# Two layer transformer on one core: the experts' first tiles among self attention's last pieces, and GpSimd's subtractions in parts

## The chip, the cores and the metric

One core of a Trainium2 chip runs the program. The time is the device time of the execution in microseconds; the median of three runs of the kernel before is 2374.72 us (2372.3 to 2374.88).

## What is computed

Two decoder layers over 8 x 256 = 2048 tokens of width 512 in float32, each sublayer followed by a residual addition and a layer norm. The change lies in the first layer, whose sublayers are:

```python
x = _layernorm(x + _L0_attn_ref(x, ...))            # power attention, 16 query heads of 128, 8 key heads
x = _layernorm(x + _L0_xattn_ref(x, ctx, ctx))      # causal cross attention, 16 heads of 32
x = _layernorm(x + _L0_ffn_ref(x, ...))             # router, 8 basis experts, shared expert

# power attention: a = (q k / sqrt(128)) ** 2, masked and gated; y = a v / sum(a); y @ Wc + bc
# _L0_ffn_ref:
gate, up = (xt @ w_gate).reshape(T, K, I), (xt @ w_up).reshape(T, K, I)      # K = 8, I = 256
basis = jax.nn.silu(gate) * up
mixed = jnp.einsum('tek,tki->tei', mix_sel, basis)                           # top 4 of 128 routes
out = ... (mixed @ w_down weighted by coeff) + silu(xt @ sgate) * (xt @ sup) @ sdown
```

The second layer is another attention, a quantised cross attention and small experts. The change doesn't touch it.

## The kernel before, in words

Every float32 product is made of three float32r products: an operand is split into a high part (a copy to float32r, mostly on ScalarE) and a low part (the operand minus its high part, on VectorE or GpSimd), and high x high, high x low and low x high are summed in PSUM (`pair3`). Names end in H and L for these parts.

Three stages of the first layer share the engines: `attention0` (A), `cross0` (C) and `experts0` (X). Each stage is a set of five generators, one for each engine, that yield after every tick. `decoder` writes an order of ticks by hand, the same for all five engines, as pairs (stage, number of ticks); `beside` mixes ticks of a second stage into those of a first. So every engine executes its instructions in that order, and semaphores tie the engines together. PSUM's eight banks are handed out in the same order, to the piece whose bank has been free longest (`Rooms`); self attention's second half and the experts' ticks before 76 use banks 0 to 3, cross attention 4 to 7. A piece waits until the last reader of its bank is done.

Self attention (A) runs 32 steps n, one per key head and quarter of 512 tokens, eight ticks each: three projections (`project`, L384), the output pieces of step n-2 in two ticks (`out`, L417, added by VectorE at L653), the attended product of step n-1 (`attend`, L434 to L439, divided at L664) with value projections now and then, the scores (L471, L473; squared at L597, multiplied with the gates at L710) and the transposition of step n-1's result (`turn`, L486; split at L605 and L722). Norms of 4 x 128 tokens are taken where their additions end: statistics (L191 to L199), Newton steps of 128x4 numbers (L203 to L213), and the apply on ScalarE (L240) or, in cross attention, on VectorE (L219). Steps 32 and 33 only finish steps 30 and 31. GpSimd makes the low parts of the weights (QKL L771, VL L791, CL L784), gates (E, L757 to L767), and residual additions (L779).

Cross attention (C) runs eight batches of 20 ticks (12 idle ticks between batch 3 and 4): scores (L953), maxima (L1069), exponentials (L1037, L1039), their transposition (`flip`, L965; copied at L1048), the product with values (L936), a last transposition (`finish`, 23 ticks behind), the product with the denominators (L1095), GpSimd's addition (L1137), and the norm.

The experts (X) run 160 tiles u of 128 tokens x (256 gate + 256 up) columns: two halves of 8 token tiles, each over ten weights (two shared, eight basis). Tile: 12 matmuls (L1289), tanh or Silu on ScalarE (L1421, L1423), two products on VectorE (L1470, L1484 or L1487); for basis weights GpSimd adds into `mixed` (L1586). Weight w is copied by ScalarE (WH, L1405) and subtracted by GpSimd (WL, L1590) at tick 8(w-1)+1; the first one at tick -5. `turn` (L1328) transposes four token tiles, split at L1436 and L1539, at ticks -2, -1, 76 and 80. Results of the shared weights and of `mixed` are transposed (`flip`, L1316, split at L1428 and L1533) and multiplied with `w_down` (`out`, L1305, added at L1528), one tick apart: the output piece is two ticks behind its tile, three for `mixed`.

The experts' buffers lie over self attention's in SBUF. Before tick -2 they use the first 32 KB, free when the last projection is done (`second_half`); at tick -2 every engine waits for all that self attention still does (`self_ends`):

```python
K.second_half = qk_mm.upto(3 * N), v_mm.upto(4 * NT)
K.self_ends = (o_mm.upto(4 * N), t_hi.upto(2 * N), o_add.upto(4 * N), e_in.upto(2 * N), ...)
```

The order around the seam is: step 31 mixed with batch 3's last ticks, step 32, X -6, step 33 up to its output pieces, X -5 to -3, the rest of step 33, X -2 to 0, then 76 experts' ticks with batches 4 to 7 beside them.

## Time and profile before

| | us |
|---|---|
| profiled execution | 2378.91 |
| its span, first to last instruction | 2377.1 |
| TensorE matmuls busy | 2108.7 (89%) |
| VectorE busy | 1305.2 (55%) |
| ScalarE busy | 1060.7 (45%) |
| GpSimd busy | 796.7 (34%) |
| mean granted TensorE clock | 0.950 of full |

The profile is one execution. A row names line, engine and operation, out<-in by the program's names, shapes and durations; behind it stands how long the engine was idle before and what ended that. PE is TensorE, DVE VectorE, ACT ScalarE, POOL GpSimd, SP SyncE. Self attention alone runs to about 450 us, with cross attention to about 850, the last steps to 900, the experts with cross attention to 1245 and alone to 1555; the second layer follows.

### The profile page before, as it was taken

The page shows a single profiled execution, that of the slowest core. Times are in us where ns is not written, and L with a number is a line of the kernel's source. Part 1 is how long each engine was busy: PE and PEld are TensorE (multiplying, and loading weights), DVE is VectorE, ACT ScalarE, POOL GpSimd, SP SyncE. Part 2 cuts the span into 40 slices and gives each one's busy share as a digit, 9 for nine tenths or more (in the row PEclk, how much of TensorE's full clock was granted, in tenths as well). Part 3 has the DMA queues.
Part 4 walks back from the last instruction along what each step waited for, and adds up shares of the span by engine and source line. Part 5 has one row for each costly group of instructions (what it writes and reads, how often), then busy time and mean ns, then how long its engine had stood idle before and what let it go on. Part 6 is the DMA issues. An engine that isn't in the chain of part 4 may idle for free.

```text
span 2377.1 us, 37602 instructions
## 1 busy us (share of the span) xinstructions
PE 2108.7 (89%) x13655; PEld 1672.7 (70%) x13669; DVE 1305.2 (55%) x3333; ACT 1060.7 (45%) x2367; POOL 796.7 (34%) x679
## 2 busy tenths in 40 slices
PE   7899999898999978999999999968999778888764
PEld 6788888687878856877777888755555367666442
DVE  2554545544465456545456411356777676777555
ACT  3332332444444424445533312145666557777632
POOL 1743533333343222134431134254445231322100
PEclk9899999899999988999999999979999889999886
DMA  3311112011012012011110011033324210000001
GB/s 132 126 36 63 45 35 73 18 58 47 27 49 62 19 36 71 25 52 48 33 50 18 18 54 74 7 52 54 61 49 62 87 41 28 15 19 6 1 10 71
DMA packets 57878, 109.03 MB, mean 46 GB/s; under 512 B 7136, under 2 KB 35040, under 8 KB 54112
## 3 DMA queue, kind: packets, MB, share of 16 engines
q1 hardware_dynamic: 57696, 106.63, 15.4%
q8 instruction: 111, 1.82, 0.3%
q14 instruction: 71, 0.58, 0.1%
HBM read 86.10 MB, written 4.26 MB: 38 GB/s over the span
## 4 chain that ended last, share of the span: by engine, by line
PE 39%; DVE 10%; issue 7%; ACT 4%; POOL 2%; SPq 1%; DMA 1%; ACTq 0%; DVEq 0%; POOLq 0%
PE PS L1289 17%; PE PS L1880 3%; PE PS L1784 3%; PE PS L1305 2%; DVE st L191 2%; ACT xP L2545 2%; DVE aM L2020 1%; PE PS L1848 1%; PE PS L953 1%; PE PS L1868 1%; PE PS L965 1%; DVE PS L2667 1%; PE PS L1835 1%; ACT xN L240 1%; PE PS L1891 1%
## 5 line engine op out<-in xcount | busy, mean ns | idle before, releaser
L1289 PE MATMUL PS<-WH,bXH 128*128 128x512 f32 x640 | 258.7, 404 | 0.0
L1289 PE MATMUL PS<-WH,bXL 128*128 128x512 f32 x640 | 250.3, 391 | 0.0
L1289 PE MATMUL PS<-WL,bXH 128*128 128x512 f32 x640 | 250.2, 391 | 0.0
L2020 DVE TENSOR_REDUCE aM<-PS 128x4 f32<-128x1024 f32 x128 | 153.8, 1221 | 55.2 <-PE PS L1848 54.0
L384 PE MATMUL PS<-aXH,QKH 128*128 128x512 f32 x384 | 158.9, 414 | 14.6 <-ACT sq L597 8.4
L1586 POOL TENSOR_TENSOR mixed<-mixed,s 128x256 f32<-128x256 f32 x112 | 82.4, 739 | 245.5 <-DVE s L1487 245.3
L1590 POOL TENSOR_TENSOR WL<-sg,WH 128x2048 fp32r<-128x2048 f32 x20 | 92.1, 4604 | 186.5 <-ACT WH L1405 186.5
L384 PE MATMUL PS<-aXH,QKL 128*128 128x512 f32 x384 | 154.3, 402 | 0.0
L384 PE MATMUL PS<-aXL,QKH 128*128 128x512 f32 x384 | 154.0, 401 | 0.0
L1959 ACT ACTIVATE aPT<-PS 128x1024 f32<-128x1024 f32 x128 | 128.6, 1024 | 49.8 <-PE PS L1868 49.0
L684 DVE TENSOR_TENSOR qkL<-PS,qkH 128x512 fp32r<-128x512 f32 x96 | 65.9, 690 | 141.1 <-ACT qkH L561 141.0
L1289 PEld LDWEIGHTS PS<-WH,bXH 128*128 128x128 f32 x640 | 120.7, 189 | 28.5 <-issue 2.0
L1289 PEld LDWEIGHTS PS<-WH,bXL 128*128 128x128 f32 x640 | 120.4, 188 | 26.5
L1289 PEld LDWEIGHTS PS<-WL,bXH 128*128 128x128 f32 x640 | 120.8, 189 | 22.8
L653 DVE TENSOR_TENSOR xN<-PS,xN 128x512 f32<-128x512 f32 x128 | 88.2, 691 | 78.7 <-PE PS L417 76.3
L2545 ACT ACTIVATE xP<-PS,xM 128x256 f32<-128x256 f32 x256 | 118.0, 482 | 29.0 <-DVE xM L2667 29.0
L710 DVE TENSOR_TENSOR aT<-sq,E 128x512 f32<-128x512 f32 (+1 forms) x128 | 84.4, 701 | 82.3 <-ACT sq L597 44.0
L757 POOL TENSOR_SCALAR E<-lgB,lgS 128x256 f32<-128x256 f32 x64 | 74.2, 1160 | 157.0 <-DVE aT L710 147.5
L1487 DVE SCALAR_TENSOR_TENSOR s<-s,cf,PS 128x256 f32<-128x256 f32 x112 | 53.9, 481 | 127.4 <-ACT s L1423 125.4
L561 ACT ACTIVATE qkH<-PS 128x512 fp32r<-128x512 f32 x96 | 57.0, 599 | 137.3 <-PE PS L384 137.3
L1470 DVE SCALAR_TENSOR_TENSOR s<-s,PS 128x256 f32<-128x256 f32 x80 | 33.7, 421 | 148.7 <-ACT s L1421 148.6
L597 ACT ACTIVATE sq<-PS 128x768 f32<-128x768 f32 x64 | 52.0, 812 | 140.4 <-PE PS L473 87.4
(395 smaller groups left out, 6038.1 us busy)
## 6 DMA issues: line engine op xcount, KB each, us to landing
sg<-in_gu SPq DMA_DIRECT2D x16, 1024.0 KB, 4.8
gQK<-in_Wqk SPq DMA_DIRECT2D x16, 768.0 KB, 6.2
gC<-in_Wc SPq DMA_DIRECT2D x16, 512.0 KB, 7.0
lgB<-gate_sums SPq DMA_DIRECT2D x32, 256.0 KB, 4.6
aqs<-aQH SPq DMA_DIRECT2D x64, 128.0 KB, 4.1
xN<-in_xT SPq DMA_DIRECT2D x4, 1024.0 KB, 11.1
xN<-in_x SPq DMA_DIRECT2D x4, 1024.0 KB, 7.7
cst<-in_cT SPq DMA_DIRECT2D x8, 512.0 KB, 4.0
```

The lines of the kernel that those rows point to most:

```text
L384: mm = e.matmul(PS[:, b, :], w[:, kc, 128 * m:128 * m + 128], x[:, kc, c:c + 512], start=kc == 0 and i == 0, stop=kc == KC - 1 and i == 2)
L653: e.tensor_tensor(xN[:, t, :], PS[:, b, :], xN[:, t, :], ALU.add).then_inc(o_add.sem, 1)
L710: at = e.tensor_tensor(aT[:, j, c:c + w].rearrange("p (h q) -> p h q", h=2), sq[:, c:c + w].rearrange("p (h q) -> p h q", h=2), E[:, j:j + ...
L757: e.tensor_scalar(E[:, j, 0:256], lgB[:, n % 2, 256 * j:256 * j + 256], lgS[:, c0:c0 + 1], 0.0, ALU.subtract, ALU.min)
L1289: mm = e.matmul(PS[:, b, :], x[:, kc, c:c + 128], y[:, kc, :], start=kc == 0 and n == 0, stop=kc == KC - 1 and n == 2)
L1586: e.tensor_tensor(mixed[:, i, :], mixed[:, i, :], s2[tick % 2][:, :], ALU.add).then_inc(t_add.sem, 1)
L1590: e.tensor_tensor(WL[w % 2][:, :, :], sg[:, :, :], WH[w % 2][:, :, :].bitcast(F32), ALU.subtract).then_inc(w_lo.sem, 1)
L1784: mm = e.matmul(PS[:, b, 0:256], w[:, kc, 128 * m:128 * m + 128], x[:, kc, :], start=kc == 0 and k == 0, stop=kc == KC - 1 and k == 2)
L1880: mm = e.matmul(PS[32 * r:32 * r + 32, b, :], V[y][:, kt, 4 * i + r, :], PT[:, (n + 2 * (r // 2) + kt) % 8, r % 2, :], start=kt == 0, stop ...
L1959: e.activation(PT[:, n % 8, :, :], PS[:, b:b + 2, :], ACTF.Exp, scale=0.25).then_inc(t_exp.sem, 1)
L2020: e.tensor_reduce(M[j % 2][:, :, :].rearrange("x q (h c) -> x h q c", h=2)[:, :, :, i], PS[:, b:b + 2, :].rearrange("p h (q k) -> p h q k" ...
L2545: last = e.activation(P[:, i % 2, a, q, :], PS[:, r, 256 * q:256 * q + 256], ACTF.Exp, bias=M[y][:, q, h:h + 1], scale=-1.0, accum_out=den ...
```

## The change

1. Self attention's buffers are laid out by when they fall free: those free after the last projection first (112,128 bytes), then the split queries and keys, free after the last scores, then gates, squares, powers and values, free after the last attended product, then the turned output and its weights. The experts' buffers are laid over them in four groups, and the common wait at tick -2 is replaced by one for each group, where it is first used: `projected`, `scored`, `attended`, `self_out`. The down weights lie in two buffers, DH[0], DH[1].
2. The order of the seam: step 31's three projections, then all of batch 3's last ticks; then step 31's rest, 32 and 33 with X -4 to 4 among them. Tiles 0 to 4 so come before self attention's end, tile 0 ahead of step 30's output pieces, tile 1 among the last attended products. The experts' first transposition is at tick -3, ahead of the last scores, the second at tick 1.
3. The first weight's split is at tick -2, between the last scores and the transposition of step 30; the second weight's at tick 5 (was 1).
4. Output pieces of the experts come one tick later behind their tiles (three, four for `mixed`), norms of the experts' tokens too (80, 84, 160; were 79, 83, 159). The stage ends two ticks later.
5. Batches 4 to 7 start five experts' ticks later and end at tick 74 instead of 73; their last ticks go in pairs. Batch 7's `finish` and statistics are behind tile 72 (were behind 69 and 70), seed and Newton steps behind tile 73 (were behind 71 and 72), the apply behind tile 74 (was 73).
6. GpSimd's low parts are made in parts: QKL, VL and WL in four, CL, DL and each half of cKL in two instructions. VL is cut to 4 x 256 columns, QKL to 4 x 384, WL to 4 x 512.

```diff
@@ -280,21 +280,24 @@
     V[0] = W("V0", [128, 8, 2, 130])
     W = Places(K, 44160)
     XH[1], XL[1] = W("aXH1", [128, KC, 1024], F32R), W("aXL1", [128, KC, 1024], F32R)
-    V[1] = W("V1", [128, 8, 2, 130])
-    gQK, gV, gC = W("gQK", [128, KC, 384]), W("gV", [128, KC, 264]), W("gC", [128, 2, 512])
-    QKH, QKL = W("QKH", [128, KC, 384], F32R), W("QKL", [128, KC, 384], F32R)
-    VH, VL = W("VH", [128, KC, 264], F32R), W("VL", [128, KC, 264], F32R)
-    CH, CL = W("CH", [128, 2, 512], F32R), W("CL", [128, 2, 512], F32R)
+    gQK, QKH, QKL = W("gQK", [128, KC, 384]), W("QKH", [128, KC, 384], F32R), W("QKL", [128, KC, 384], F32R)
+    gV, VH, VL = W("gV", [128, KC, 264]), W("VH", [128, KC, 264], F32R), W("VL", [128, KC, 264], F32R)
+    bc = W("bc", [128, 512])
+    lg, lz, l1, UT = W("lg", [128, NT * 8]), W("lz", [128, NT * 8]), W("l1", [128, NT * 8]), W("UT", [128, 128])
+    assert W.at == K.floor + 112128
     qkH, qkL = W("qkH", [128, 3, 512], F32R), W("qkL", [128, 3, 512], F32R)
+    assert W.at == K.floor + 124416
     E = W("E", [128, 2, 384])
     sq = W("sq", [128, 768])
     aT = W("aT", [128, 2, 768])
+    V[1] = W("V1", [128, 8, 2, 130])
+    assert W.at == K.floor + 145024
     yN = W("yN", [128, 2, 2, 2, 128])
+    gC, CH, CL = W("gC", [128, 2, 512]), W("CH", [128, 2, 512], F32R), W("CL", [128, 2, 512], F32R)
     yH, yL = W("yH", [128, 2, 512], F32R), W("yL", [128, 2, 512], F32R)
-    lg, lz, l1 = W("lg", [128, NT * 8]), W("lz", [128, NT * 8]), W("l1", [128, NT * 8])
-    UT, DM = W("UT", [128, 128]), W("DM", [128, 2, 128])
+    assert W.at == K.floor + 169600
+    DM = W("DM", [128, 2, 128])
     lgS, lgR, lgB = W("lgS", [128, NT * 8]), W("lgR", [128, 128]), W("lgB", [128, 2, 512])
-    bc = W("bc", [128, 512])
     nr, nr2 = W("nr", [128, 2, 2, 1]), W("nr2", [128, 2, 2, 1])
     xst = [xN[:, 4 * p:4 * p + 4, :] for p in range(NP)]
@@ -768,8 +771,9 @@
                 if n % 2 and n // 2 + 1 < 16:
                     e.wait_ge(*in_qk.upto(n // 2 + 2))
                     e.wait_ge(*qk_hi.upto(n // 2 + 2))
-                    e.tensor_tensor(QKL[:, :, :], gQK[:, :, :], QKH[:, :, :].bitcast(F32),
-                                    ALU.subtract).then_inc(qk_lo.sem, 1)
+                    for kc in range(KC):
+                        last = e.tensor_tensor(QKL[:, kc, :], gQK[:, kc, :], QKH[:, kc, :].bitcast(F32), ALU.subtract)
+                    last.then_inc(qk_lo.sem, 1)
             yield
             if n < NP:
...
@@ -851,8 +857,8 @@
         yield
 
     K.first_half = qk_mm.upto(3 * 16), v_mm.upto(before[4]), y_mm.upto(2 * 16)
-    K.second_half = qk_mm.upto(3 * N), v_mm.upto(4 * NT)
-    K.self_ends = (o_mm.upto(4 * N), t_hi.upto(2 * N), o_add.upto(4 * N), e_in.upto(2 * N), c_lo.upto(16), y_mm.upto(2 * N), t_lo.upto(2 * N))
+    K.projected = qk_mm.upto(3 * N), v_mm.upto(4 * NT), residual.upto(NT)
+    K.scored, K.attended, K.self_out = s_mm.upto(2 * N), y_mm.upto(2 * N), o_mm.upto(4 * N)
     return Stage(8 * (N + 2) + 3, banks, tensor, scalar, vector, gpsimd, sync)
 
...
-    U, first, last = 160, -6, 163
-    outs = [(80 * h + 8 * k + i, 80 * h + 8 * k + i + (3 if k == 9 else 2), i, c, z)
-            for h in (0, 1) for z, (k, c) in enumerate(((0, 2), (1, 4), (9, 0))) for i in range(8)]
+    U, first, last = 160, -4, 165
+    outs = [(80 * h + 8 * k + i, 80 * h + 8 * k + i + (4 if k == 9 else 3), i, z)
+            for h in (0, 1) for z, k in enumerate((0, 1, 9)) for i in range(8)]
     out_at, flip_at = {}, {}
-    for v, (u, at, i, c, z) in enumerate(outs):
+    for v, (u, at, i, z) in enumerate(outs):
         out_at.setdefault(at, []).append(v)
     route_at, choose_at, gate_at, coef_at, mix_at = {}, {}, {}, {}, {}
     for p in range(NP):
         base, q = 80 * (p // 2), p % 2
@@ -1205,13 +1221,13 @@
             gate_at[base + 3 + 4 * q + k] = p, k
         choose_at[base + 2 + 4 * q] = p
         coef_at[base + 10 + 2 * q], mix_at[base + 11 + 2 * q] = p, p
-    split_at = {-5: 0}
-    for w in range(1, 20):
+    split_at = {-2: 0, 5: 1}
+    for w in range(2, 20):
         split_at[8 * (w - 1) + 1] = w
-    down_at = {0: 0, 4: 1, 12: 2}
+    down_at = {2: 0, 4: 1, 12: 2}
     norm_at = {}
     for p in range(NP - 1):
-        n = 79 + 80 * (p // 2) + 4 * (p % 2)
+        n = 80 + 80 * (p // 2) + 4 * (p % 2)
         norm_at.update({n: ("stats", p), n + 1: ("newton", p), n + 2: ("apply", p)})
     loads = [12 * (w // 10) + (2 * (w % 10) + 2 if w % 10 < 2 else w % 10 + 3) for w in range(20)]
 
...
@@ -1370,9 +1387,6 @@
             mm.then_inc(f_mm.sem, 1)
 
         for tick in range(first, last):
-            if tick == -2:
-                for x in old:
-                    e.wait_ge(*x)
             if 0 <= tick < U:
                 tile(tick)
@@ -1393,23 +1407,25 @@
 
     def scalar(e):
         for tick in range(first, last):
-            if tick == -5:
+            if tick == -2:
                 e.wait_ge(*in_r.upto(1))
                 e.activation(rH[:, :, :], dst[:, :, :].rearrange("p a c -> p (a c)")[:, 0:512].rearrange(
                     "p (k c) -> p k c", k=KC), ACTF.Copy).then_inc(r_hi.sem, 1)
             if tick in split_at:
                 w = split_at[tick]
                 e.wait_ge(*in_w.upto(loads[w]))
-                if w >= 2:
+                if w == 1:
+                    e.wait_ge(*self_out)
+                elif w:
                     e.wait_ge(*t_mm.upto(8 * (w - 1)))
                 e.activation(WH[w % 2][:, :, :], sg[:, :, :], ACTF.Copy).then_inc(w_hi.sem, 1)
-            if tick == -2:
-                for x in old:
-                    e.wait_ge(*x)
             if tick in down_at:
-                k, c = down_at[tick], (2, 4, 0)[down_at[tick]]
+                k = down_at[tick]
+                a, c = k // 2, 2 * (k % 2)
+                if k == 0:
+                    e.wait_ge(*attended)
                 e.wait_ge(*in_d.upto(k + 1))
-                e.activation(DH[:, c:c + 2, :], dst[:, :, :], ACTF.Copy).then_inc(d_hi.sem, 1)
+                e.activation(DH[a][:, c:c + 2, :], dst[:, :, :], ACTF.Copy).then_inc(d_hi.sem, 1)
             if tick in norm_at and norm_at[tick][0] == "apply":
                 norms[norm_at[tick][1]].apply_act(e)
             if 0 <= tick < U:
...
@@ -1469,6 +1484,8 @@
             if by_tanh(u):
                 step(e.scalar_tensor_tensor(out=s1[z][:, :], in0=s1[z][:, :], scalar=1.0, in1=gate, op0=ALU.add, op1=ALU.mult))
             if k < 2:
+                if u < 2:
+                    e.wait_ge(*scored)
                 if u >= 80 and k == 0 and i < 2:
                     e.wait_ge(*t_add.upto(added(u - 2)))
                 elif u % 80 >= 2:
...
@@ -1587,13 +1597,16 @@
             if tick in split_at:
                 w = split_at[tick]
                 e.wait_ge(*w_hi.upto(w + 1))
-                e.tensor_tensor(WL[w % 2][:, :, :], sg[:, :, :], WH[w % 2][:, :, :].bitcast(F32),
-                                ALU.subtract).then_inc(w_lo.sem, 1)
+                for kc in range(KC):
+                    last_ = e.tensor_tensor(WL[w % 2][:, kc, :], sg[:, kc, :], WH[w % 2][:, kc, :].bitcast(F32), ALU.subtract)
+                last_.then_inc(w_lo.sem, 1)
             if tick in down_at:
-                k, c = down_at[tick], (2, 4, 0)[down_at[tick]]
...
@@ -1611,22 +1624,20 @@
 
         for tick in range(first, last):
             if tick == first:
-                for x in second_half:
+                for x in projected:
                     e.wait_ge(*x)
                 e.dma_start(dst[:, :, :].rearrange("p a c -> p (a c)")[:, 0:512].rearrange("p (k c) -> p k c", k=KC),
                             d["wr"]).then_inc(in_r.sem, 16)
                 fetch(0)
-            if tick == -4:
+            if tick == -1:
+                e.wait_ge(*scored)
+                e.dma_start(am[:, :, :], d["amp"]).then_inc(in_am.sem, 16)
+                e.dma_start(es[:, :], d["es"].rearrange("(n a) -> n a", a=1)).then_inc(in_am.sem, 16)
                 e.wait_ge(*r_hi.upto(1))
                 e.wait_ge(*r_lo.upto(1))
                 down(0)
                 e.wait_ge(*w_lo.upto(1))
                 fetch(1)
-            if tick == -2:
-                for x in old:
-                    e.wait_ge(*x)
-                e.dma_start(am[:, :, :], d["amp"]).then_inc(in_am.sem, 16)
-                e.dma_start(es[:, :], d["es"].rearrange("(n a) -> n a", a=1)).then_inc(in_am.sem, 16)
             if tick in down_at and down_at[tick] < 2:
                 e.wait_ge(*d_lo.upto(down_at[tick] + 1))
                 down(down_at[tick] + 1)
...
@@ -3116,13 +3127,13 @@
         step = [(1, 3), (1, 3), (1, 3), (1, 3), (1, 3), (1, 3), (1, 2), (1, 1)]
         pair = [(2, 8), (1, 5), (2, 3)]
         order = [(0, 1), (A, 1 + 8 * 17 + 4), (C, 11)]
-        late = beside(order, A, step[4:] + 14 * step + [(5, 6), (1, 3), (2, 1)], C, 16 * pair + 3 * [(3, 3)])
-        order += [(X, 1), (A, 5), (X, 3), (A, 5)]
+        late = beside(order, A, step[4:] + 13 * step + [(3, 9)], C, 16 * pair + 3 * [(3, 3)])
         order += [(C, n) for n, _ in late]
-        order += [(X, 2)]
-        late = beside(order, X, 76 * [(1, 3)], C, [(3, 3)] + 16 * [(2, 6), (1, 3), (2, 3)] + 9 * [(1, 3)])
+        order += [(X, 1), (A, 2), (X, 1), (A, 2), (X, 1), (A, 1), (X, 2)]
+        order += [(A, 5), (X, 1), (A, 3), (X, 1), (A, 5), (X, 1), (A, 3), (X, 1), (A, 2)]
+        late = beside(order, X, 72 * [(1, 3)], C, [(3, 3)] + 16 * [(2, 6), (1, 3), (2, 3)] + 4 * [(2, 3)] + [(1, 3)])
         order += [(C, n) for n, _ in late]
-        order += [(X, 163 - 76)]
+        order += [(X, 169 - 9 - 72)]
         order += [(i, 1) for i in range(4, 7)]
         assert [sum(n for s, n in order if s == i) for i in range(7)] == [s.ticks for s in stages]
 
```

## Rows read from the trace of the kernel before

**Rows 1.** Busy time by windows: window, its us, each engine's busy us, PEclk, DMA, GB/s.
```profile
848.20:949.20 101.00, 74.99 (x378) 62.03 (x378) 64.47 (x175) 33.41 (x64) 24.18 (x13) 0.86 0.20 62
862.00:917.20 55.20, 35.27 (x160) 29.64 (x159) 35.00 (x92) 16.63 (x25) 4.55 (x1) 0.75 0.10 30
1238.00:1250.00 12.00, 8.00 (x27) 6.10 (x26) 7.10 (x9) 0.77 (x2) 4.74 (x3) 0.72 0.27 89
1281.00:1291.00 10.00, 7.05 (x28) 5.44 (x27) 3.40 (x7) 4.79 (x11) 0.00 (x0) 0.83 0.29 104
```

**Rows 2.** Timeline of TensorE, 855 to 945: start, duration, operation, [idle before, releaser].
```profile
861.73 0.68 PE L434 MATMUL PS<-V,aT 128*128 128x129 f32 x4 [4.49 <-DVE xN L653]
...
873.81 0.76 PE L417 MATMUL PS<-CH,yH 128*128 128x512 f32 x1 [3.34 <-issue]
874.38 0.63 PE L417 MATMUL PS<-CL,yH 128*128 128x512 f32 x1
...
890.67 0.77 PE L417 MATMUL PS<-CH,yH 128*128 128x512 f32 x1 [3.60 <-issue]
...
912.44 3.67 PE L1328 MATMUL PS<-idF,xN 128*128 128x128 f32 x16 [10.31 <-DVE bXL L1539]
...
917.18 0.39 PE L1289 MATMUL PS<-WH,bXH 128*128 128x512 f32 x1
```

**Rows 3.** Timelines of ScalarE, GpSimd and VectorE: the first splits of the experts.
```profile
895.89 1.90 ACT L1405 ACTIVATE WH<-sg 128x2048 fp32r<-128x2048 f32 x1
...
897.86 4.55 POOL L1590 TENSOR_TENSOR WL<-sg,WH 128x2048 fp32r<-128x2048 f32 x1 [36.98 <-ACT WH L1405]
...
899.90 3.06 DVE L1516 TENSOR_TENSOR rL<-dst,rH 128x512 fp32r<-128x512 f32 x1
```

**Rows 4.** Timelines of TensorE and VectorE, 843 to 873: steps of the chain.
```profile
844.33 0.28 PE L953 MATMUL PS<-cKH,cQL 32*128 32x256 f32 x2
...
847.40 0.82 PE L965 MATMUL PS<-idF,cP 128*128 128x128 f32 x6
849.82 0.86 PE L936 MATMUL PS<-cPT,cV 128*32 128x256 f32 x16 [1.60 <-ACT cPT L1048]
...
864.11 1.92 DVE L219 TENSOR_SCALAR xN<-xN,mv,ny 128x512 f32<-128x512 f32 x4
...
867.09 0.50 PE L471 MATMUL PS<-qkH 128*128 128x512 f32 x1 [0.81 <-DVE yN L664]
...
871.38 1.03 DVE L710 TENSOR_TENSOR aT<-sq,E 128x512 f32<-128x512 f32 x2 [0.93 <-issue]
```

**Rows 5.** Two lines of the program: instructions, shortest/median/longest ns, first and last start.
```profile
L1129 POOL TENSOR_TENSOR cKL<-cst,cKH x16: 1270/1291/1321, 428.4 to 1155.5; 128x512 fp32r<-128x512 f32 x16
...
L240 ACT ACTIVATE xN<-xN,nc,ny x54: 797/799/817, 417.1 to 2372.0; 128x512 f32<-128x512 f32 x54
```

**Rows 6.** Timelines of VectorE and GpSimd at the second seam.
```profile
1235.45 6.58 DVE L219 TENSOR_SCALAR xN<-xN,mv,ny 128x512 f32<-128x512 f32 x4
...
1275.48 4.54 DVE L213 SCALAR_TENSOR_TENSOR ny<-nb,ny 128x4 f32<-128x4 f32 x1
...
1236.55 4.74 POOL L1590 TENSOR_TENSOR WL<-sg,WH 128x2048 fp32r<-128x2048 f32 x1
```

**Rows 7.** What TensorE waited for, 916 to 1545: us in total, times, longest.
```profile
PE PS L1305 <- DVE s L1487: 4.0, 1, 4.0
PE PS L1305 <- issue: 3.3, 2, 2.9
PE PS L1305 <- DVE tL L1533: 2.6, 2, 1.5
```

**Rows 8.** Timeline of TensorE behind the experts' last tile.
```profile
1541.78 0.47 PE L1305 MATMUL PS<-DH,tH 128*128 128x512 f32 x1 [1.15 <-DVE tL L1533]
```

**Rows 9.** What TensorE waited for, 45 to 847: us in total, times, longest.
```profile
PE PS L434 <- DVE aT L710: 6.1, 2, 6.0
...
PE PS L384 <- POOL QKL L771: 3.9, 1, 3.9
```

More of the change, by code:

```diff
@@ L1308, in flip @@
         def flip(v):
-            u, _, i, c, z = outs[v]
+            u, _, i, z = outs[v]
             b, left = rooms["e_flip", v]
@@ L1513, in vector @@
         for tick in range(first, last):
-            if tick == -5:
+            if tick == -2:
                 e.wait_ge(*r_hi.upto(1))
@@ L1578, in gpsimd @@
         for tick in range(first, last):
-            if tick == -2:
-                for x in old:
-                    e.wait_ge(*x)
             if 0 <= tick < U and parts(tick)[1] > 2:
```

73 lines of the change are left out of this document (42 added, 31 removed).

## The prediction

> **What bounds the kernel now.** I read the busy table and the 40 slices first: TensorE is busy 89% of the span, nearly solid in the slices that hold self attention and the experts. So inside them only two things matter: TensorE's waits, and the time it works at the lower clock. The table by windows then shows where they sit. From 848.2 us (self attention's last projection done) to 949.2 us (the experts' tile 6 starts) TensorE is busy 75.0 of 101.0 us, with a mean clock of 0.86 [rows 1]. The waits, 26.0 us, all lie before 916 us: the rows show 4.49, 3.34, 3.60 and 10.31 us, the smaller ones make up the rest [rows 2, 4]. Between 862.0 and 917.2 us the granted clock is 0.75 on average, so 27.6 us of 55.2 ran at 1.2 GHz [rows 1]; some 7.5 of these lie inside waits, the other 20 cost half, 10 us. A 512-column matmul is shown with 0.63 us there and 0.39 us at 2.4 GHz; its starts lie 0.20 us further apart, so time doubles [rows 2]. This first seam thus costs 36 us; that is all the reordering can win there.
>
> What ends the waits is latency, not load: VectorE alone normalises, splits and adds in program order, and TensorE's next piece stands behind a PSUM bank or a split that VectorE or GpSimd owes.
>
> A second seam is where cross attention ends and the second half of the tokens begins. TensorE waits 4.0 us at 1239.4 and 2.9 at 1282.7 [rows 7], and runs at a mean clock of 0.72 and 0.83 in the 12 and 10 us around them [rows 1], which is 6.7 and 3.4 us at 1.2 GHz, nearly all of it work, so 3.4 and 1.7 us lost. A further wait of 1.5 us follows [rows 7]. The causes are in [rows 6]: VectorE's normalising of four tiles takes 6.58 us instead of 1.92 [rows 4], while GpSimd's 4.74 us subtraction runs, and a 128x4 operation takes 4.54 us.
>
> **The change, part by part.** The memory order itself executes nothing; it permits the new order of pieces. The new order, worked on the clock of the old trace:
>
> 1. Three projections now run back to back and end at 844.6 instead of 847.4. Cross attention's last pieces follow without cover. Transposing exponentials waits for them: from the scores' last matmul to that transposition the chain takes 2.9 us; the old trace hides it behind a projection, and shows its neighbour bare, 1.60 us [rows 4]. I count waits of 1.3, 2.8, 1.0 and 0.6 us, against 1.6 before.
> 2. The normalisation after them now stands whole ahead of the four additions. Denominator product, GpSimd's two additions, statistics, Newton steps and the apply (1.92 us) end at 863.7 by the old trace's steps; that trace has two of the four additions earlier. The experts' transposition wants those banks: waits of 2.3 and 0.4 us, then 1.5 for its split, against 4.49 [rows 2]. Scores start at 871.0 instead of 867.1 and the powers end 5.3 us later, as they did [rows 4], at 876.3.
> 3. ScalarE gets the router's and first expert weight's high parts between the squares and self attention's transposed output: 0.5 and 1.9 us, at 875.1 to 877.5. GpSimd's low part follows; in four parts of 1.29 us [rows 5] it ends at 882.8. Tile 0 is ahead of the four output pieces in TensorE's order, so everything waits for it: TensorE has nothing after 874.4, a wait of 8.4 us. Queued behind it are the output pieces, behind those the additions and the next normalisation. In the old order the same split was hidden under output pieces, but TensorE then waited 10.31 us for the first tile [rows 2, 3].
> 4. Tiles 0 to 4, a transposition and the router product then fill what were waits of 3.60 and 10.31 us. I lay out 0.3 + 1.2 us (split, product with the denominators) and 1.3 us (third low part, behind VectorE's statistics). At tile 6 ScalarE first applies a normalisation of four tiles (4 x 0.80 us, overlapping to 2.9) and takes the second weight (1.9) [rows 3, 5] ahead of the activation of tile 5, which frees tile 6's bank: 4.3 us.
>
> SyncE is passed too: the first weights' transfers are issued by 856 and wanted at 875; the next by 883 and wanted at 934. The work of these 19 and 51 us hides them; without it each would cost its time to land. The new waits on scored and attended are satisfied before they are reached in the tensor order.
>
> Sum of the first seam: waits of 25.4 us instead of 26.0; at 1.2 GHz I put 7.8 us lost instead of 10, as the waits are of the same kind. With rounding of the work between, a gain of 3.5 us. Bounds: no loss of clock at all, gain 11; all of it at 1.2 GHz (rival 2), loss 8.
>
> 5. Second seam. The outputs come a tick later after their tiles. That hides the waits of 2.9 and 1.5 us with the 1.7 us of clock of the first: 6.1 us won, of which I take 6. Against it, cross attention's last group now has quotient and statistics in one tick, and the ten small operations of the Newton steps come right behind the start of GpSimd's subtraction. I read the stalls as whole instructions waiting for whole instructions: the split of the router's weights ended 0.55 us after GpSimd's subtraction that began before it [rows 3]. In parts, each small operation can then meet its own part: four stalls of 1.29 us instead of one of 4.4. So the wait of 4.0 us becomes 6.6: 2.5 lost. Bounds for the stall: none (small operations slip between the parts), to four full parts, 5.2 us. I take the far end because the next part is already queued. Sum: a gain of 3.5 us.
>
> 6. The tail of the stage has one more output piece exposed behind the last tile. Its price is the wait of the first such piece, 1.15 us [rows 8]; 3.0 at most, the next one's. Loss 1.2.
>
> 7. Parts elsewhere. At the start TensorE waits 6.1 us for powers that GpSimd held up and 3.9 us for a weight's low part [rows 9]. Most of the first is behind residual additions that stay whole. The second grows with three more instruction starts: four parts of 2048 columns cost 4 x 1.29 instead of 4.55 [rows 3, 5], 0.2 us a start, 0.6 in all. Elsewhere stalls on the powers get shorter (a group at 430 us by about 1 us). I take these as nothing together, -1.5 to +1.5. The other subtractions have a whole step of cover; without it each costs its 0.6 us.
>
> GPSIMD Engine Reference (section 8) of the Trainium skill says GpSimd shares its SBUF interfaces with VectorE instructions that have two SBUF inputs or run in a 2-port mode; that fits which operations stall here, but it calls it contention and gives no order of service. If the interface were shared evenly, parts would change nothing at either seam and step 5 would give a gain of 6 us instead of 3.5.
>
> Sum: -3.5 - 3.5 + 1.2 + 0 = -5.8, taken as -6.0 us. The profiled execution took 2378.9 us (span 2377.1), giving 2372.9; the median of the runs is 2374.7, 4.2 lower, so I predict 2368.7 us.
>
> **Rivals.**
> 1. The gaps fill better: the spread waits let the clock stay at 2.4 GHz through the first seam (7.8 us) and the small operations slip between parts (2.5). Then 2368.7 - 10.3 = 2358.4. For it: short waits like the 1.60 us at 849.8 [rows 4] may be too short to lower it. Against: waits of 3.3 and 3.6 us were each accompanied by 1.2 GHz work [rows 2].
> 2. Slower: the clock. Between 849 and 883 us TensorE would be busy half of the time only, in short pieces. If it is granted 1.2 GHz through that stretch and tiles 0 and 1, some 24 us of work take double. Half of this is in the chain, as transposition, attending, scores, tile 0 and outputs are: 12 us more, 2380.7. It decides the sign once more than about 20 us of busy work in the new seam runs at 1.2 GHz. For it: 0.75 over the old seam with TensorE busy 64% of it [rows 1].
> 3. The move does nothing, since each wait moved reappears behind the same chain, and the parts bring what they cost: 2374 (both seams within 1 us).
>
> **Chances.** Forecast 0.50 (its own range 2362 to 2375), rival 1 0.17, rival 2 0.18, rival 3 0.15. About 0.2%, 4.7 us, is what a measurement can tell from no change; the bound for faster is 2370.0. The forecast's case lies below it with 0.32 of its 0.50. Faster 0.32 + 0.17 = 0.49; slower is rival 2 less its small outcomes and the forecast's tail, 0.19; same 0.32. The range 2357 to 2380 leaves out the ends of rivals 1 and 2.
>
> **What would show it.** Right: tile 0 starts 7 to 10 us after TensorE's transposition of the attended output, released by GpSimd; about 25 us of waits between the last projection and tile 6; a wait of 4 us before tile 6 behind ScalarE; the output piece at the second seam waits over 5 us, and the wait near 1283 is gone. Wrong: a mean clock in that stretch above 0.95 or below 0.8; small VectorE operations at most once delayed per subtraction; tile 0 held by something ahead of the weight's low part.

## The result, and the profile of the changed kernel

The changed kernel took 2381.53 us (median of 6 runs, 2378.61 to 2384.86), the kernel before 2373.11 us (6 runs beside them): a ratio of 1.0033, with a 95% interval of 1.0022 to 1.0045. It is slower, by 8 us, where 6 us less were forecast; the time lies outside the range. A second comparison gave 1.0033 again (1.0020 to 1.0046; 2380.27 against 2372.88 us).

The profiled execution of the changed kernel took 2378.61 us (span 2376.4), that of the kernel before 2378.91. So two profiles of equal length stand for medians 8 us apart, and the first thing to settle was which trace is typical. The busy table and the granted clock by slices, after:

```profile
span 2376.4 us, 37748 instructions
PE 2105.4 (89%) x13655; PEld 1667.8 (70%) x13669; DVE 1295.1 (54%) x3333; ACT 1062.1 (45%) x2367; POOL 820.7 (35%) x836
PEclk9899999899999979999999999979999989999886
```

GpSimd is busy 24 us longer, with 157 more instructions: the parts. The first seam by windows (window, its us, busy us of each engine, PEclk, DMA, GB/s), to be read against the first row of [rows 1]:

```profile
848.00:944.00 96.00, 73.51 (x350) 59.40 (x351) 56.89 (x155) 29.79 (x52) 21.05 (x17) 0.86 0.17 49
```

The mean clock is the 0.86 of before, and a quarter of the time is waits as before. What TensorE waited for from 846 to 945 us (total, times, longest):

```profile
PE PS L1305 <- POOL WL L1601: 8.2, 1, 8.2
PE PS L1305 <- DVE s L1501: 3.5, 1, 3.5
PE PS L971 <- ACT cP L1045: 2.7, 1, 2.7
PE PS L1322 <- issue: 2.2, 1, 2.2
PE PS L1345 <- DVE xN L656: 2.2, 1, 2.2
PE PS L942 <- ACT cPT L1054: 1.0, 1, 1.0
```

The biggest is tile 0's wait for the first weight's low part, where [rows 2] had 10.31 us for the first tile's tokens. The chain behind it, in ScalarE's, GpSimd's and TensorE's timelines:

```profile
876.95 1.90 ACT L1421 ACTIVATE WH<-sg 128x2048 fp32r<-128x2048 f32 x1
...
878.93 4.93 POOL L1601 TENSOR_TENSOR WL<-sg,WH 128x512 fp32r<-128x512 f32 x4 [12.01 <-ACT WH L1421]
...
884.12 0.77 PE L1305 MATMUL PS<-WH,bXH 128*128 128x512 f32 x1 [8.24 <-POOL WL L1601]
```

The second seam, VectorE's, GpSimd's and TensorE's timelines from 1236 us; this answers to [rows 6, 7]:

```profile
1236.85 0.16 DVE L203 TENSOR_SCALAR ny<-nv 128x4 int32<-128x4 int32 x1
...
1237.77 5.01 POOL L1601 TENSOR_TENSOR WL<-sg,WH 128x512 fp32r<-128x512 f32 x4
1237.87 1.21 DVE L213 SCALAR_TENSOR_TENSOR ny<-nb,ny 128x4 f32<-128x4 f32 x1
...
1239.11 1.22 DVE L210 TENSOR_TENSOR na<-ny 128x4 f32<-128x4 f32 x1
...
1240.36 1.22 DVE L211 SCALAR_TENSOR_TENSOR nb<-na,nv 128x4 f32<-128x4 f32 x1
...
1241.62 1.18 DVE L213 SCALAR_TENSOR_TENSOR ny<-nb,ny 128x4 f32<-128x4 f32 x1
...
1242.84 0.16 DVE L210 TENSOR_TENSOR na<-ny 128x4 f32<-128x4 f32 x1
...
1248.01 0.77 PE L1322 MATMUL PS<-DH,tH 128*128 128x512 f32 x1 [6.44 <-issue]
```

Four operations of 128x4 numbers take 1.2 us each while a part runs, 0.16 us when none does, and TensorE stands 6.44 us. What it waited for from 1228 to 1320 us:

```profile
PE PS L1322 <- issue: 6.4, 1, 6.4
PE PS L1322 <- DVE tL L1546: 3.1, 3, 1.5
PE PS L1367 <- ACT mixed L1459: 0.6, 1, 0.6
```

The waits of 2.9 and 1.5 us of [rows 7] are gone; in their place stand one of 0.6 and three of 3.1 us in all.

### The traces side by side

For every kernel run I cut the trace at the same pieces of TensorE's work: start of self attention's steps 2 and 31 (first projection), of the experts' tiles 8, 72 and 82, and of the second layer's first matmul. Each cell is TensorE's waits in the stretch (the sum of its gaps over 0.1 us; a gap that ends at a cut is counted once, in the stretch ahead of the cut, and the idle time ahead of the first matmul isn't counted), and the stretch's length, in us; the difference is work at either clock. "Seams" is step 31 to the second layer, where every kernel does the same work in another order. A cell inside the seams can hold a piece that another order has elsewhere; their sum can't.

| kernel | median | to step 2 | to step 31 | to tile 8 | to tile 72 | to tile 82 | to layer 2 | seams | to the end |
|---|---|---|---|---|---|---|---|---|---|
| before, first trace | 2373.11 | 11.4 / 79.2 | 28.8 / 755.5 | 26.0 / 126.1 | 0.5 / 267.3 | 4.0 / 51.7 | 19.4 / 283.9 | 49.9 / 729.0 | 813.5 |
| before, again | 2373.15 | 11.7 / 78.7 | 28.5 / 753.0 | 25.6 / 124.8 | 0.5 / 267.3 | 4.0 / 51.1 | 17.5 / 283.9 | 47.6 / 727.1 | 811.5 |
| after | 2381.53 | 13.1 / 80.4 | 28.6 / 754.9 | 24.1 / 117.0 | 1.4 / 274.2 | 6.4 / 52.7 | 20.3 / 285.5 | 52.2 / 729.4 | 811.7 |
| after, again | 2380.27 | 13.0 / 79.4 | 29.0 / 755.4 | 24.3 / 116.9 | 1.4 / 274.1 | 6.4 / 52.7 | 20.2 / 285.5 | 52.4 / 729.3 | 812.7 |
| parts_only | 2368.34 | 13.0 / 80.5 | 28.8 / 755.2 | 22.4 / 121.1 | 0.5 / 267.2 | 1.7 / 47.2 | 19.2 / 282.1 | 43.8 / 717.7 | 813.4 |
| order_only | 2386.93 | 11.6 / 77.8 | 27.6 / 752.7 | 23.2 / 119.1 | 4.3 / 280.3 | 6.6 / 54.0 | 20.8 / 287.4 | 55.0 / 740.7 | 812.1 |
| tail_pairs | 2378.87 | 12.7 / 80.6 | 28.9 / 755.5 | 22.4 / 120.9 | 0.5 / 266.2 | 6.0 / 54.2 | 19.4 / 283.5 | 48.3 / 724.9 | 814.0 |
| late_outputs | 2367.6 | 13.0 / 80.0 | 29.5 / 755.3 | 24.5 / 118.9 | 0.9 / 269.4 | 0.0 / 43.5 | 20.5 / 285.6 | 46.0 / 717.3 | 813.2 |
| spread_tail | 2373.41 | 12.0 / 79.8 | 29.5 / 756.7 | 24.5 / 118.4 | 1.3 / 274.1 | 1.4 / 46.8 | 17.9 / 285.5 | 45.0 / 724.9 | 810.7 |
| tile0_behind | 2371.7 | 13.1 / 80.7 | 28.6 / 755.4 | 17.4 / 109.5 | 1.6 / 274.4 | 6.5 / 53.0 | 18.3 / 285.5 | 43.8 / 722.4 | 809.6 |
| weights_parts | 2364.8 | 10.6 / 78.4 | 29.3 / 752.4 | 24.0 / 122.0 | 0.5 / 267.2 | 1.7 / 47.2 | 17.2 / 283.7 | 43.4 / 720.1 | 810.7 |
| both_moved | 2367.11 | 13.3 / 79.6 | 30.2 / 756.8 | 17.5 / 110.4 | 1.7 / 274.4 | 1.3 / 46.8 | 20.1 / 285.5 | 40.6 / 717.1 | 811.4 |
| best_mix | 2365.27 | 10.4 / 79.2 | 30.0 / 755.7 | 17.7 / 110.4 | 1.5 / 274.3 | 1.3 / 46.8 | 20.0 / 285.5 | 40.6 / 717.0 | 812.3 |

The first trace of before is a long draw: it has 2.9 us more up to step 31, 1.9 in the seams and 2.0 behind them than its repetition, though nothing differs. The prediction had taken 4.2 us off for that, as the runs allowed; but it read the places to be won from the long draw too.

### The profile page after: what moved, and what is told of

Read it like the earlier page. It is cut to its first block, busy times and chain, and to the rows that moved or that the text cites. A ratio compares the mean times of both kernels' runs of the same rounds, so it can differ in the third digit from the quotient of the medians.

```text
span 2376.4 us, 37748 instructions
## 1 busy us (share of the span) xinstructions
PE 2105.4 (89%) x13655; PEld 1667.8 (70%) x13669; DVE 1295.1 (54%) x3333; ACT 1062.1 (45%) x2367; POOL 820.7 (35%) x836
## 4 chain that ended last, share of the span: by engine, by line
PE 40%; DVE 10%; issue 7%; ACT 5%; POOL 2%; DMA 0%; SPq 0%; DVEq 0%; ACTq 0%; POOLq 0%
PE PS L1305 17%; PE PS L1795 3%; PE PS L1891 3%; PE PS L1322 2%; ACT xP L2556 2%; DVE aM L2031 2%; DVE st L191 2%; PE PS L1859 1%; PE PS L959 1%; PE PS L971 1%; ACT xN L240 1%; PE PS L2408 1%; PE PS L1879 1%; PE PS L1846 1%; DVE PS L2678 1%
## 5 line engine op out<-in xcount | busy, mean ns | idle before, releaser
L1305 PEld LDWEIGHTS PS<-WH,bXH 128*128 128x128 f32 x640 | 121.1, 189 | 42.0 <-issue 10.4
L1970 ACT ACTIVATE aPT<-PS 128x1024 f32<-128x1024 f32 x128 | 128.5, 1024 | 48.4 <-PE PS L1879 47.6
L1601 POOL TENSOR_TENSOR WL<-sg,WH 128x512 fp32r<-128x512 f32 x80 | 100.9, 1294 | 136.7 <-ACT WH L1421 136.7
L1305 PEld LDWEIGHTS PS<-WH,bXL 128*128 128x128 f32 x640 | 121.1, 189 | 26.8
L713 DVE TENSOR_TENSOR aT<-sq,E 128x512 f32<-128x512 f32 (+1 forms) x128 | 81.6, 678 | 82.5 <-ACT sq L600 43.8
```

Source lines behind the costliest of these rows:

```text
L713: at = e.tensor_tensor(aT[:, j, c:c + w].rearrange("p (h q) -> p h q", h=2), sq[:, c:c + w].rearrange("p (h q) -> p h q", h=2), E[:, j:j + ...
L1305: mm = e.matmul(PS[:, b, :], x[:, kc, c:c + 128], y[:, kc, :], start=kc == 0 and n == 0, stop=kc == KC - 1 and n == 2)
L1601: last_ = e.tensor_tensor(WL[w % 2][:, kc, :], sg[:, kc, :], WH[w % 2][:, kc, :].bitcast(F32), ALU.subtract)
L1970: e.activation(PT[:, n % 8, :, :], PS[:, b:b + 2, :], ACTF.Exp, scale=0.25).then_inc(t_exp.sem, 1)
```

## The experiments

Every kernel was timed beside the kernel before, whose median was 2372.88, 2373.5 and 2372.86 us in the three comparisons. The names are those of the table.

### The two kernels once more

No edit.

> The kernel before, unchanged, as a control. Theory A (the change is slower by what it does, some 6 to 8 us): this stays at 1.000 of the kernel before, and its profile shows the waits of the old trace (26 us in the first seam, 4.0 and 2.9 us in the second); the profiled time of the old trace, 2378.9 against a median of 2373.1, was a high draw of one execution. Theory B (the times scatter by several us between programs and executions, and the profiled pair, 2378.9 and 2378.6, tells the truth): this lands anywhere between 0.998 and 1.003.

> The changed kernel again, on one chip with the other three. Theory A: 1.002 to 1.0045 of the kernel before, 2378 to 2384 us. Theory B: 0.998 to 1.003, with executions that scatter over more than 6 us.

The ratios are 1.000 (0.9991 to 1.0009) and 1.0033. The loss is real, and 0.1% either way can be told from none.

### The parts alone, the order alone

parts_only is the kernel before with part 6 of the change; order_only is the changed kernel with every subtraction whole again, for the experts' weights:

```diff
-                for kc in range(KC):
-                    last_ = e.tensor_tensor(WL[w % 2][:, kc, :], sg[:, kc, :], WH[w % 2][:, kc, :].bitcast(F32), ALU.subtract)
-                last_.then_inc(w_lo.sem, 1)
+                e.tensor_tensor(WL[w % 2][:, :, :], sg[:, :, :], WH[w % 2][:, :, :].bitcast(F32),
+                                ALU.subtract).then_inc(w_lo.sem, 1)
```

> The kernel before with only GpSimd's subtractions in parts; order, memory and all else as before. If the parts are what costs (Theory P): slower by 4 to 8 us, with about 24 us more of GpSimd's busy time and VectorE's small operations at the second seam delayed four times by about 1.2 us each. If the order costs (Theory O): within 1.5 us of the kernel before, since the stalls are as long in sum as they were; at the start of self attention TensorE waits some 2 us longer for the second weights' low part (5.7 instead of 3.9 us).

> The changed kernel with GpSimd's subtractions whole again; the new order and memory stay. Theory O: slower than the kernel before by 4 to 8 us, as the changed kernel is. Theory P: faster than the kernel before by about 3 us, the first seam's gain. In both, TensorE's wait for tile 0 is about 0.6 us shorter than the 8.24 us of the changed kernel, and at the second seam one Newton operation takes 4.4 us instead of four at 1.2.

Parts alone: 2368.34 us, 0.998 (0.997 to 0.9991). Order alone: 2386.93 us, 1.0058 (1.0045 to 1.0071). So the order costs 12 us with the parts (2380.3 against 2368.3) and 14 us without (2386.9 against 2373.1), and the parts bring 5 to 7 in either. One half of the change pays, and the other costs twice that. Neither expectation had the parts as a gain, or an order that costs more than 8 us. Without parts the new order is also longer between tiles 8 and 72 (280.3 us against 274.1): TensorE waits 4.0 us there for a query's low part (cQL), with a spell at 1.2 GHz behind it.

The parts' gain at the second seam, in the old order, shows in VectorE's and TensorE's timelines of parts_only; [rows 6, 7] have 6.58 and 4.0 us here:

```profile
1231.35 4.28 DVE L219 TENSOR_SCALAR xN<-xN,mv,ny 128x512 f32<-128x512 f32 x4
...
1237.02 0.47 PE L1309 MATMUL PS<-DH,tH 128*128 128x512 f32 x1 [1.70 <-DVE s L1491]
```

With the wait at 1.7 us the clock didn't fall there at all, as windows of parts_only around both of the seam's places show, against the 0.72 and 0.83 of [rows 1]:

```profile
1228.00:1252.00 24.00, 22.30 (x111) 18.30 (x110) 16.72 (x34) 6.62 (x14) 10.03 (x10) 1.00 0.14 45
1266.00:1290.00 24.00, 21.27 (x101) 17.24 (x100) 15.77 (x28) 10.30 (x18) 5.02 (x4) 1.00 0.12 45
```

At the second seam of order_only, the subtraction is whole, the Newton steps meet it once, and TensorE waits as long as with parts:

```profile
1241.21 4.53 DVE L213 SCALAR_TENSOR_TENSOR ny<-nb,ny 128x4 f32<-128x4 f32 x1
1245.77 0.16 DVE L210 TENSOR_TENSOR na<-ny 128x4 f32<-128x4 f32 x1
...
1241.12 4.61 POOL L1596 TENSOR_TENSOR WL<-sg,WH 128x2048 fp32r<-128x2048 f32 x1
...
1251.55 0.77 PE L1318 MATMUL PS<-DH,tH 128*128 128x512 f32 x1 [6.63 <-issue]
```

6.63 us with one stall of 4.5, 6.44 us with four of 1.2: the parts have no share in this wait. It is there because the new order puts the last group's steps in one unbroken row, behind the subtraction's start.

### The end of cross attention in pairs: taken alone, and taken back

tail_pairs is parts_only with one line of the old order changed; spread_tail is the changed kernel with its line changed the other way (the rest of the experts' order adjusted to the same count of ticks, the third transposition's banks kept apart four ticks longer):

```diff
-        late = beside(order, X, 76 * [(1, 3)], C, [(3, 3)] + 16 * [(2, 6), (1, 3), (2, 3)] + 9 * [(1, 3)])
+        late = beside(order, X, 76 * [(1, 3)], C, [(3, 3)] + 16 * [(2, 6), (1, 3), (2, 3)] + [(2, 18)] + 3 * [(2, 3)] + [(1, 3)])
```

```diff
-        late = beside(order, X, 72 * [(1, 3)], C, [(3, 3)] + 16 * [(2, 6), (1, 3), (2, 3)] + 4 * [(2, 3)] + [(1, 3)])
+        late = beside(order, X, 75 * [(1, 3)], C, [(3, 3)] + 16 * [(2, 6), (1, 3), (2, 3)] + 2 * [(2, 3)] + 5 * [(1, 3)])
```

> The kernel before with GpSimd's subtractions in parts, and of the new order only the end of cross attention: its last nine ticks wait and go in pairs, so that quotient and statistics follow tile 70 or 72 together and the Newton steps meet the weight's subtraction. Everything else, first seam and output distance too, is as before. Theory T (this placement is what loses the second seam): the output piece there, which waits 1.7 us with parts alone, waits 5 to 7 us, the spell at 1.2 GHz returns, and the time rises by 5 to 8 us over parts alone (2368.3), to 2373 to 2377. Theory F (the loss sits in the first seam): within 2 us of 2368.3.

> The changed kernel with cross attention's last five ticks one by one, behind tiles 72 to 76 instead of 72 to 74; the experts take eight banks from tick 80 instead of 76. Theory T: Newton steps and apply then come after the weight's subtraction, the wait of 6.45 us at the second seam falls below 3 us, its spell at 1.2 GHz shortens, and the time falls by 4 to 7 us to 2373 to 2376. Theory F: no change beyond 1.5 us. Counter: fewer banks until tick 80 could turn the win into waits for banks.

tail_pairs: 2378.87 us, 1.0022 (1.0013 to 1.0032), 10.5 us over parts_only; spread_tail: 2373.41 us, 0.9999 (0.999 to 1.0007), 6.9 us under the changed kernel. Between tiles 72 and 82 one is 7.0 us longer, the other 5.9 us shorter. TensorE's timeline of tail_pairs, then of spread_tail:

```profile
1241.52 0.76 PE L1309 MATMUL PS<-DH,tH 128*128 128x512 f32 x1 [6.00 <-DVE s L1491]
1242.08 0.63 PE L1309 MATMUL PS<-DL,tH 128*128 128x512 f32 x1
1242.51 0.63 PE L1309 MATMUL PS<-DH,tL 128*128 128x512 f32 x1
```

```profile
1245.55 0.47 PE L1322 MATMUL PS<-DH,tH 128*128 128x512 f32 x1 [1.36 <-DVE s L1504]
```

After the 6.00 us the matmuls start 0.43 us apart, at 1.2 GHz; after 1.70 and 1.36 us the clock stays up. So the placement costs 6.9 us in the new order and 10.5 in the old, where 5 to 8 were expected: it is the cause of some 7 of the order's 12 us, shown from both sides.

### Later outputs alone

late_outputs is parts_only with the outputs and norms of the changed kernel:

```diff
-    U, first, last = 160, -6, 163
-    outs = [(80 * h + 8 * k + i, 80 * h + 8 * k + i + (3 if k == 9 else 2), i, c, z)
+    U, first, last = 160, -6, 165
+    outs = [(80 * h + 8 * k + i, 80 * h + 8 * k + i + (4 if k == 9 else 3), i, c, z)
...
-        n = 79 + 80 * (p // 2) + 4 * (p % 2)
+        n = 80 + 80 * (p // 2) + 4 * (p % 2)
```

> The kernel before with parts, and of the change only the experts' output pieces and norms one tick later. By the prediction's steps 5 and 6 this hides the waits of 2.7 and 1.5 us at the second seam and costs 1.2 us at the tail: 2 to 3 us faster than parts alone (2368.3). The rival, read from the changed kernel's trace, where 0.6 + 1.2 + 1.5 + 0.5 us of waits stand in their place: no gain there and 1.4 us at the tail, so 1 to 3 us slower than parts alone.

2367.6 us, 0.997 (0.9959 to 0.998): 0.7 us under parts_only, which the two intervals can't tell from nothing, so neither expectation held. It does hide the wait of 1.7 us at the second seam, and the 2.73 and 1.46 us behind it become four of 3.95 us in all. Of these 1.9 us, 0.5 come back at tile 11 and 1.7 behind tile 160, where one more piece is exposed: from tile 8 to the second layer TensorE waits 21.4 us in parts_only and 21.5 here. What it waited for from 1222 to 1310 us:

```profile
PE PS L1309 <- DVE tL L1537: 3.4, 3, 1.7
PE PS L1354 <- ACT mixed L1448: 0.6, 1, 0.6
```

### Tile 0 behind the output pieces

tile0_behind is the changed kernel with two pieces of self attention's tail drawn ahead of tile 0:

```diff
-        order += [(X, 1), (A, 2), (X, 1), (A, 2), (X, 1), (A, 1), (X, 2)]
-        order += [(A, 5), (X, 1), (A, 3), (X, 1), (A, 5), (X, 1), (A, 3), (X, 1), (A, 2)]
+        order += [(X, 1), (A, 2), (X, 1), (A, 3), (X, 2)]
+        order += [(A, 5), (X, 2), (A, 3), (X, 1), (A, 5), (X, 1), (A, 3), (X, 1), (A, 2)]
```

> The changed kernel with tile 0 behind step 30's output pieces and the first weight's split behind step 30's transposition. If the prediction's step 3 is right (tile 0 holds TensorE 8.2 us while output pieces lie ready): the wait falls to 1 to 4 us, with less work at 1.2 GHz, and the time falls by 4 to 9 us to 2371 to 2376. If the chain behind the split is what counts and only its place changes: the wait appears ahead of the second tile or the next attended product, and the time stays within 2 us of 2380.3.

2371.7 us, 0.9992 (0.9984 to 1.0001), 8.6 us under the changed kernel. In place of the 8.24 us TensorE's timeline has a wait in front of the output pieces. The profile names no releaser for it; the turned output's low part, which these pieces need, ends on VectorE (L725) 0.2 us earlier, at 879.49:

```profile
879.70 0.77 PE L420 MATMUL PS<-CH,yH 128*128 128x512 f32 x1 [3.17 <-issue]
```

The stretch to tile 8 is 7.4 us shorter. Waits make up 6.9 of that: 5.1 at tile 0, and 1.6 at tile 6, whose wait falls from 3.55 to 1.90.

### Both mended, and parts only where they pay

both_moved is the changed kernel with the edits of spread_tail and tile0_behind. best_mix is both_moved with QKL, VL and CL whole again. weights_parts is the kernel before with only WL in parts, three lines in all:

```diff
-                e.tensor_tensor(WL[w % 2][:, :, :], sg[:, :, :], WH[w % 2][:, :, :].bitcast(F32),
-                                ALU.subtract).then_inc(w_lo.sem, 1)
+                for kc in range(KC):
+                    last_ = e.tensor_tensor(WL[w % 2][:, kc, :], sg[:, kc, :], WH[w % 2][:, kc, :].bitcast(F32), ALU.subtract)
+                last_.then_inc(w_lo.sem, 1)
```

> The changed kernel with both faults of its order mended: tile 0 behind two more output pieces, and the end of cross attention spread over the first tiles of the experts. Alone these gave 8.6 and 6.9 us. If the two losses are independent places, the sum is 2380.3 - 8.6 - 6.9 = 2364.8 us, 31 to tile 8 takes 110 us and tiles 72 to 82 take 47 us. Then the new order costs nothing against the old one with the same parts (2368.3) and may be 3 us better. Rival, each gain was partly the luck of where the clock's slow spells fell, and they don't add: 2368 to 2372. Rival, the order costs by something else (its four more tiles of work at the second seam, the later outputs at the end): 2367 to 2370 with both seams as short as forecast.

> As the run with both faults mended, but with self attention's three subtractions (QKL, CL, VL) whole as in the kernel before; parts stay in cross attention and the experts. By my account of self attention this takes another 3.5 us off: 2361.3 us (2359 to 2365), steps 0 to 2 back at 39.2 and 24 to 28 at 121.5 us. Rival, these segments' difference is not due to the parts: the same time as with all parts. Rival, whole subtractions put the first seam's longer stalls back because CL lies beside its last steps: 31 to tile 8 longer by 1 to 2 us, total 2363.

> The kernel before with one edit: the weight subtraction WL of the experts in four parts, everything else whole, old order. My account: of the parts' net gain (2368.3 against 2373.1) self attention gave back 3.5 us (steps 0 to 2 1.4 us longer, steps 24 to 28 2.1 us longer) because the shorter stalls of VectorE moved GpSimd's results later there, and the two seams gained 3.7 and 3.9 us, all of it from WL. So self attention returns to 39.2 and 121.5 us while the seams keep 121.1 (31 to tile 8) and 47.3 us (tiles 72 to 82): 2373.1 - 3.7 - 3.9 - 1.8 (tiles 82 to 88) = 2363.7 us; with the 2 us by which two profiles of one kernel differ, 2362 to 2367. Rival, self attention's 3.5 us are scatter of single profiles and not the parts: 2368 as with all parts. Second rival, part of the seam gain came from the parts of KL and DL: above 2367, with the first seam longer than 122 us.

both_moved: 2367.11 us, 0.9983 (0.9973 to 0.9993); the two mendings add nearly up (15.5 forecast, 13.2 found). The seams are as short as expected (110.4 and 46.8 us), so the missing 2.3 us fit the last rival too, a small cost elsewhere in the order. With them the new order costs nothing against the old one (parts_only 2368.34), and brings nothing that can be told: the seams are 717.1 us long against 717.7. It waits less, 40.6 us against 43.8, but works longer, 676.5 against 673.9.

best_mix: 2365.27 us, 0.9969 (0.9957 to 0.9981); weights_parts: 2364.8 us, 0.9967 (0.9956 to 0.9978). Forecast were 3.5 us for making self attention's subtractions whole; found were 1.8 in the new order, where the two intervals overlap, and, with KL and DL whole too, 3.5 in the old. What the traces show cleanly is the start. In the five kernels that have QKL whole, TensorE waits 10.4 to 11.7 us up to step 2, and step 0 to step 2 takes 39.1 to 39.4 us; in the eight with parts it waits 12.0 to 13.3 and takes 40.6 to 41.1. From step 2 to step 31 the waits don't tell them apart (27.6 to 30.0 us whole, 28.6 to 30.2 in parts), and the lengths hardly (752.4 to 755.7, 754.9 to 756.8). Most of what differs there is one stretch at 1.2 GHz: step 25 to 26 takes 30.5 to 30.6 us at a mean clock of 0.94 in four of the five, and 31.9 to 32.3 at 0.89 to 0.90 in all others, with 2.6 to 2.8 us of waits in every one. weights_parts is among those others, though it executes the same instructions up to there as the kernel before: of its forecasts, 39.2 us came true (39.2), 121.5 for steps 24 to 28 didn't (123.0). The subtraction ahead of step 2 in GpSimd's timeline, in parts (after, again) and whole (before, again):

```profile
74.73 4.48 POOL L775 TENSOR_TENSOR QKL<-gQK,QKH 128x384 fp32r<-128x384 f32 x4 [0.70 <-ACT QKH L578]
```

```profile
75.18 3.42 POOL L771 TENSOR_TENSOR QKL<-gQK,QKH 128x1536 fp32r<-128x1536 f32 x1 [0.67 <-ACT QKH L575]
```

TensorE waits for its end: 5.7 us instead of 3.9 (2.8 to 3.9 us in the five kernels, 4.6 to 7.1 in the eight). The 1.06 us between the two aren't the three more starts alone. With nothing of VectorE's beside them four such parts take 3.92 us (at 112.04 in the same trace), against 3.50 whole, 0.14 a start. At step 2 VectorE's products of squares and gates (L713) get in between: the four parts take 0.99, 1.44, 1.17 and 0.98 us, and some 0.6 us are GpSimd's own waiting for VectorE.

The lowest median, that of weights_parts (best_mix can't be told from it), is thus that of the old order with one of the six kinds of subtraction in parts: 8 us under before, 16 under the changed kernel.

## Why the prediction was wrong

**Steps 1 to 4, the first seam: held, nearly wait by wait.** Counted were 1.3, 2.8, 1.0, 0.6, 2.3, 8.4 and 4.3 us; the trace has 0.99, 2.74, 1.01, 0.65, 2.16, 8.24 and 3.55. In all 25.4 us were counted and 24.1 found. The mean clock over it stayed at 0.86: some 27 us of the 96 at 1.2 GHz (0.14 x 96 x 2) against 28 of 101. So rivals 1 and 2 fell, and so did the 2.2 us that the clock was to give; 0.7 us of the 3.5 forecast were called rounding of the work between, and no run shows them. Against the repeated trace the seam has 1.3 us less waiting. And the sum hid what the runs then showed: the parts alone shorten this seam by 3.2 us of waits (25.6 to 22.4), so the new order with them is 1.9 us of waits worse than the old with them. Step 3's wait was priced rightly and taken as unavoidable; nothing asked what tile 0 behind the output pieces would give. It gives 8.6 us.

**Step 5, the second seam: the wait's size held, its cause and the credit failed.** The wait came out at 6.44 us against 6.6. Its cause didn't: four stalls of parts instead of one whole was to cost 2.5 us, and order_only has the wait at 6.63 with one whole stall. The order made it, and the parts by themselves made the old wait of 4.0 us 1.7: set against that, the paired end lost 4.7 us of waiting and a stretch at 1.2 GHz, not 2.5. Nor does the 2.5 follow from the stalls that were counted, 4 x 1.29 us for one of 4.4, which is 0.8 longer, so that 6.6 was met is partly luck. The credit of 6 us is the step that failed. It took the later outputs to hide the waits of 2.9 and 1.5 us; after the seam, TensorE waits 20.3 us to the second layer where it had 17.5 (again) to 19.4 (first trace). The waits of 2.9 and 1.5 us became 0.56, 1.16, 1.52 and 0.46, which is 0.7 us less and not 4.4, and late_outputs, the move by itself, is worth 0.7 us. The clock's 1.7 of the 6 us were won where they were looked for, 1.00 against the 0.83 of [rows 1]. But the longer wait has its own stretch at 1.2 GHz, 6.9 us of it (0.51 in the first window), as the first trace of before had there (6.8); the repeated trace had 3.5:

```profile
1244.00:1251.00 7.00, 2.99 (x8) 2.34 (x9) 4.55 (x10) 0.39 (x1) 2.35 (x3) 0.51 0.50 150
1280.00:1290.00 10.00, 8.28 (x40) 6.25 (x39) 5.10 (x18) 5.50 (x9) 0.00 (x0) 1.00 0.32 105
```

So a gain of 3.5 us was forecast for this seam, and the paired end of cross attention cost about 7. By the prediction's own terms the new order was to win 8.3 us (3.5 + 6 - 1.2) and the parts to lose 2.5. It lost 12 to 14, and they won 5 to 7: both signs were wrong, and the total is off by 14 us, less than the order's 20, because the two errors partly cancel. The signs named for a right forecast came all the same (GpSimd released tile 0 after 8.24 us, 3.55 us of waiting ahead of tile 6, 6.44 at the second seam, 0.56 left near 1283): they test the waits of the new order, and not what the old order does with parts.

**Step 6, the tail: the exposed piece held.** One more at 1.15 us was counted; the trace shows 1.15, 1.15, 3.00 and 1.94 us, where before (again) has 1.16, 3.00 and 1.69. The stretch from tile 82 to the second layer is 1.6 us longer than before in both traces, close to the 1.2 forecast, but part of it is a moved piece.

**Step 7, the parts elsewhere: mis-sized.** Taken as nothing, with 1.5 us either way; the waits up to step 31 grew from 40.1 to 42.0 us (repeated runs), and all of it is the wait at step 2, 3.90 to 5.75. A start cost 0.14 us in QKL and 0.13 in WL (4.93 us for the four against the 4.55 of [rows 3]), where 0.2 was taken; what was left out is that VectorE's instructions get in between the parts and put off the last one's end. Step 2 starts at 79.4 to 80.7 us in the eight kernels with parts, at 77.8 to 79.2 in the five without: 1.5 us later on average, where 0.6 were counted. Steps 2 to 31 are 2.4 us longer in the repeated runs, with waits of 28.5 and 29.0 us, so most of it is work at the lower clock. At the seams, where the prediction had counted nothing in favour of parts, they won 3.2 and 2.3 us of waits, and the clock at the second.

**The waits between.** From tile 8 to 72 nothing was forecast; 0.9 us of waits came. Sum of waits from step 31 to the second layer: 47.6 before, 52.4 after; work at either clock 679.5 and 676.9; so 2.1 us slower in the seams. With 3.0 us up to step 31 and 1.2 behind the seams (the second layer is the same program, so scatter) the repeated traces differ by 6.4 us in span, near to the medians' 7.1.

**What misled.** The long draw made the seam's old cost 1.4 us too dear and hid self attention's loss: the first trace's 755.5 us for steps 2 to 31 are matched by the changed kernel's 754.9, while the repetition has 753.0.

**Left open.** Whether parts lengthen self attention beyond step 2 isn't shown: the kernels with parts have a longer stretch at 1.2 GHz around step 25 with the same waits, but weights_parts has it without parts there. Nor is it shown which of the small waits of the new order (0.9 between tiles 8 and 72, 0.6 to 3 at the tail) could be ordered away: both_moved still has them. That the clock was low around the long waits of the second seam (3.99 to 6.63 us) and stayed up around the short ones (1.33 to 1.70) holds in all these runs, but no run changed the wait alone. Between them it went both ways: around the wait of 2.73 us ahead of an output piece 40 us later, tail_pairs and weights_parts have 3.4 us at 1.2 GHz, and parts_only has none.

## What to carry to other kernels

When a reordering puts a piece that waits for a long chain ahead of work that is ready, price the swap of the two as well as the wait: here one pair of lines was worth 8.6 us, and spreading a stage's last ticks singly instead of in pairs 7. Price a wait against the best form of the old order, too: part of the old wait was the whole subtraction's, and went away without any reordering. Cut a GpSimd instruction into parts where VectorE's operations on the path run beside it, and leave it whole where its own end is waited for. Take a second profile of the kernel before as soon as one lies several us above the median, before reading small gains from it.
